# One-hots of a segment sum made one block earlier in a graph layer on one core

## What is computed

```python
h = node_features @ W_node.T + b_node
e = edge_features @ W_edge.T + b_edge
msg = (h[src] + e) @ W_msg.T + b_msg
s = segment_sum(msg, dst, num_segments=n)
deg = segment_sum(ones, dst, num_segments=n)
x = layernorm(x + s / maximum(deg, 1.0)[:, None])
```

## Time and profile before

| | us |
|---|---|
| median of 3 runs | 785.0 (783.43 to 785.41) |
| the profiled execution, its own time | 783.87 |
| its span, first to last instruction | 782.0 |
| TensorE busy (matmul) | 688.6 |
| VectorE busy | 630.1 |
| ScalarE busy | 438.3 |
| GpSimd busy | 270.0 |

### The profile page before, as it was taken

How to read it: one execution, slowest core, us unless ns; L and a number is a source line. 1 busy time by engine, 2 the same in 40 slices (tenths; PEclk the granted TensorE clock), 3 DMA queues, 4 the chain that set the end, 5 groups by cost and what they waited for, 6 DMA issues and landing times.

```text
span 782.0 us, 24842 instructions
## 1 busy us (share of the span) xinstructions
PE 688.6 (88%) x10360; PEld 620.7 (79%) x10360; DVE 630.1 (81%) x1155; ACT 438.3 (56%) x897; POOL 270.0 (35%) x210
## 2 busy tenths in 40 slices
PE   3265577899999989999999998999999999999995
PEld 3244466778888979989988987988998998989994
DVE  7989896868998878878878877789798788779822
ACT  3322496656565556556556555656665665656641
POOL 2737300301443836426426455532543542000000
PEclk9998698999999999999999999999999999999998
DMA  6953543434556574474472575464574574454000
GB/s 174 321 182 79 138 135 111 167 111 146 183 190 194 187 260 156 160 258 158 159 262 55 184 253 195 152 229 156 194 238 146 192 236 153 173 182 169 17 14 16
DMA packets 81518, 130.71 MB, mean 167 GB/s; under 512 B 12100, under 2 KB 25126, under 8 KB 81303
## 3 DMA queue, kind: packets, MB, share of 16 engines
q1 hardware_dynamic: 73230, 115.79, 44.3%
q0 software_dynamic: 7200, 12.39, 5.7%
q10 hardware_dynamic: 974, 0.90, 0.5%
HBM read 125.80 MB, written 3.23 MB: 165 GB/s over the span
## 4 chain that ended last, share of the span: by engine, by line
PE 52%; DVE 11%; issue 4%; POOL 2%; DMA 1%; DVEq 1%; ACT 0%; POOLq 0%
PE x_ps L745 29%; PE count_ps L730 10%; PE win_ps L666 8%; DVE key_hot L886 3%; DVE row_hot L886 2%; PE win_ps L673 2%; POOL x_gathered L607 2%; DMA x_gathered<-in_x_dram,x_index 1%; PE misc_ps L761 1%; PE misc_ps L762 1%; DVE y L932 1%; DVEq L863 1%; DVE y L925 1%; DVE onehot L852 1%; DVE sums_e L876 1%
## 5 line engine op out<-in xcount | busy, mean ns | idle before, releaser
L1416 ACT CAST region<-count_ps 128x490 bf16<-128x490 f32 x575 | 324.3, 573 | 192.8 <-PE count_ps L730 188.5
L745 PE MATMUL x_ps<-region,x_rest 128*128 128x250 bf16 x2254 | 413.6, 270 | 0.0
L745 PE MATMUL x_ps<-region,x_hi 128*128 128x250 bf16 x1127 | 306.2, 272 | 0.5 <-ACT region L1416 0.5
L607 POOL DMA_INDIRECT x_gathered<-in_x_dram,x_index x144 | 195.1, 1355 | 278.5 <-PE count_ps L730 258.9
L886 DVE TENSOR_TENSOR row_hot<-iota_bf,row 125x3200 bf16<-125x3200 bf16 x115 | 209.4, 1821 | 42.1 <-PE count_ps L730 29.1
L730 PE MATMUL count_ps<-key_hot,row_hot 125*128 125x98 bf16 x2875 | 224.4, 209 | 15.2 <-ACT region L1416 8.6
L745 PEld LDWEIGHTS x_ps<-region,x_rest 128*128 128x128 bf16 x2254 | 211.4, 98 | 16.2
L730 PEld LDWEIGHTS count_ps<-key_hot,row_hot 125*128 125x128 bf16 x2875 | 185.6, 99 | 37.9 <-issue 10.4
L886 DVE TENSOR_TENSOR key_hot<-iota_bf,key 125x2500 bf16<-125x2500 bf16 x115 | 167.2, 1454 | 0.0
L666 PE MATMUL win_ps<-edges,onehot 128*32 128x128 f32 x3232 | 107.2, 286 | 13.7 <-DVE onehot L852 12.1
L745 PEld LDWEIGHTS x_ps<-region,x_hi 128*128 128x128 bf16 x1127 | 109.5, 97 | 8.0 <-ACT region L1416 0.6
(11 more groups left out here) (194 smaller groups left out, 415.7 us busy)
## 6 DMA issues: line engine op xcount, KB each, us to landing
edges<-in_edge_attr_dram SPq DMA_DIRECT2D x101, 1024.0 KB, 5.8
resid<-in_x_dram SPq DMA_DIRECT2D x25, 125.0 KB
out_dram<-y SPq DMA_DIRECT2D x25, 125.0 KB
x_gathered<-in_x_dram,x_index POOLq DMA_INDIRECT x144
region<-in_dst_dram ACTq DMA_DIRECT2D x1, 768.0 KB
win_src<-in_src_dram,clipped_int POOLq DMA_INDIRECT x23, 4.4
x_index<-in_src_dram SPq DMA_DIRECT2D x9, 8.0 KB, 5.7
region<-in_L_gnn_W_node_dram SPq DMA_DIRECT2D x1, 64.0 KB
```

Source lines behind the costliest of these rows:

```text
L607: pool.indirect_dma_start(out=x_gathered[:, i, :], out_offset=None, in_=x[:, :], in_offset=bass.IndirectOffsetOnAxis(ap=x_index[:, k, i:i ...
L745: mm = pe.matmul(x_ps[m % 2][:, 0:NB], rows, counts[m % 2][:, b, :], start=(n == 0), stop=(n == PARTS - 1))
L1416: act.copy(counts[m % 2][:, :, f * FILL * 2:(f + 1) * FILL * 2], count_ps[fill % COUNT_BANKS][:, 0:FILL * KEYS].rearrange("p (n b) -> p b ...
```

## The change

In VectorE's list, the limit up to which a segment makes one-hots goes from two blocks past the segment's last one to three, in all segments from u = LEAD on. In the five segments of the lead-in it stays as it was. The number of buffers, the waits written into `make_onehot` and everything else are unchanged.

```diff
@@ -1186,7 +1186,7 @@
                     placed[0] += 1
                 if n is not None:
                     take_stats(n)
-                while ts and hot[0] < min(NS, ts[-1] + ONEHOT_SLOTS):
+                while ts and hot[0] < min(NS, ts[-1] + 1 + (ONEHOT_SLOTS if u >= LEAD else ONEHOT_SLOTS - 1)):
                     make_onehot(hot[0])
                     hot[0] += 1
                 if n is not None:
```

## The result

The changed kernel takes 779.0 us (median of 5 runs, 778.87 to 781.72) where the kernel before, here of five runs too, takes 785.0. By these medians 6.0 us are gained where 9.0 were forecast, and the time lies inside the range of 773.4 to 779.6, at its upper end. The ratio of the two kernels, 0.9940 with a 95% interval of 0.9919 to 0.9962, is that of their means, 779.8 and 784.5 us: 4.7 us gained, which would put the time at 780.3, just above the range. The profiled execution is the slowest of the five, 781.72 us, so by the profiles alone the gain is 783.87 - 781.72 = 2.15 us.

A forecast was written before the change was run, and what follows sets the result against it. TensorE was taken to bound the kernel from 162 us on. Gain 9.7 us less 0.7 for the early one-hot makes 9.0: 783.87 becomes 774.9, plus 1.1 for the median gives 776.0, range 773.4 to 779.6.

The forecast's parts named there:

- What bounds the kernel: From 162 to 775 us TensorE, busy 591.8 of 613 us; before that, other waits hold the kernel.
- (a): VectorE's raised limit makes one-hots earlier, so TensorE's nine one-hot waits at source blocks, 12.1 us, disappear.
- (b): In VectorE's one-hot loop the raised limit adds no wait, so nothing is queued behind a new one.
- The seven places: Source blocks where gathered rows have room: the full one-hot waits are gained, 12.1 - 1.38 - 1.04 = 9.7 us.
- Rival 1: VectorE's additions hide behind the one-hot at seven places: some 3.5 us lost, 779.5; 8 in 100.
- The early one-hot: The third one-hot in the first pair's segment delays L1213, for which TensorE waits: costs 0.7 us, between 0 and 2.2.
- I count both at nothing: Two source blocks where TensorE also awaits gathered rows: waits merge to 2.11 and 2.64 us, no gain.
- Rival 3: Merged waits at two places each bring a half-clock stretch: 1.7 to 3.3 us lost each, about 781; 6 in 100.
- rival 2: All nine places give their full wait, gathers at two coming relatively earlier: 2.4 us more, 773.6; 5 in 100.
- rival 4: Half clock after the merged waits lasts 20 us, as at 73 to 93 us: 796, slower; 3 in 100.
- rival 5: The awaited one-hot is still the late one; only the early 0.7 us is left: 785.7; 4 in 100.
- TensorE's busy time within 1 us: Sign in the next profile: TensorE's busy time, 688.6 us before, is unchanged within 1 us.

The follow-up runs named there:

- after_2: The changed kernel measured once more, on a chip of the quicker sort, against the kernel before: 778.9 us against 785.77, ratio 0.9920.
- selective_2: The changed kernel, but with the old one-hot limit around source blocks 1 and 5, against the kernel before: 778.81 us, ratio 0.9907.
- onehot_later: The changed kernel with the higher one-hot limit only from round 3 on, against the kernel before: 780.13 us, ratio 0.9927.

## Why the prediction was wrong, point by point

- What bounds the kernel, and (a), right: TensorE from 162 us on; the nine waits for one-hots, 12.1 us, are gone, every one.
- (b) No new wait behind the limit: right. No wait for additions or second-level sums appeared, and VectorE's busy time is 629.4 against 630.1.
- The seven places, 9.7 us: right, 9.9 by the rounds. Rival 1 (the additions) did not happen: nothing waits in their place.
- The early one-hot, 0.7 us: right. The three one-hots stand in one row of 4.87 us (some 5 forecast), and the wait for L1213 is 9.1 (9.2).

```profile
81.61 4.87 DVE L852 TENSOR_TENSOR onehot<-iota_bf,rel_col 128x512 f32<-128x512 bf16 x3
```

- The step that failed is "I count both at nothing". Its working was that the gathers end where they ended and TensorE merely waits for them longer: 2.11 and 2.64 us. The prediction's sum lets these two places gain nothing and lose nothing; they lost 3.9 to 7.4 us. The working held for the landing (5.27 us after the last issue, in the row below, against 5.37 in the earlier trace rows) and not for the issues ahead of it. The chain of waits, 272 to 280 us:

```profile
272.34 1.07 POOL x_gathered L607
273.40 0.30 issue
273.71 5.27 DMA x_gathered<-in_x_dram,x_index
```

  The 16 issues became 1.37 us longer, since TensorE's release moved against VectorE. I had read in the earlier trace rows that GpSimd is released by TensorE's counts, and had seen that its issues vary from 0.94 to 2.2 us, but took the variation as given. It depended on the very phase that the change shifts. The waits were 3.45 and 3.57 us. That the extra 1.37 us are gathers that meet one-hots is read from the rows of each gather; no run took it away by the release alone.
- Rival 3 was given 6 in 100 and came true: the clock fell at both places in the first profile, for 6.9 us each, up to 3.05 and 2.65 us lost, and at one in after_2, for 3.4 us, 1.7 lost. Its price of 1.7 to 3.3 us a place was right; its sum was not, since 6.6 us on top of 776.0 is up to 782.6 and not 781. I had the clock at 1.00 after 2.09 us and at 0.50 after 4.53 and put merged waits of 2.1 and 2.6 on the safe side. With waits of 3.5 us there was no safe side; and selective_2 shows that even 1.42 and 1.26 us, 1 us apart, were not on it. The length of the wait doesn't decide alone, since 3.18 and 3.31 us kept the clock; what does is not shown. The chance was too low for a wait that lay between the two rows.
- The two together take 3.9 us (after_2) to 7.4 us (the first profile) of the 9.0 forecast, and leave 5.1 to 1.6; the medians say 6.0 and 6.9. Within the 1 to 2 us by which runs differ that is the whole of the shortfall. That the median still lies in the range is luck: the range was left wide for the spread of runs and for rivals 1 and 2, and neither happened. Rivals 2, 4 and 5 did not happen: no stretch of 20 us at half clock came into the late stage. The early stage of this execution has one that the kernel before doesn't show (49.6 to 70.1 us), but round 5 begins only 0.7 us later, so it cost next to nothing.
- "TensorE's busy time within 1 us": wrong, 4.6 more, which is the half clock seen from the other side. It is all in the stretch from 162 to 775 (596.6 against 591.8 in the earlier trace rows).

## What to carry to other kernels

When a wait is removed from one engine, its signals come earlier against every other engine: for each queue that they release, look at what runs there at the new time, and take no instruction's length as fixed if it varied in the trace before. Where the removed wait stood ahead of another one, add the two, and if the sum lies between a wait that kept the clock and one that lost it, price the half clock as likely. Then give room to what is late next (here source blocks further apart), and the first gain comes whole.

## What the runs showed of the hardware

- A gather issued by GpSimd while VectorE is inside a wide one-hot, an operation with two SBUF inputs, ended 0.81 to 0.83 us after it in 118 of 131 cases (before and changed kernel). A free one takes 0.94 us. Of the 195 us of gathers in the kernel before, 144 x 0.94 = 135 would be free time; 57 of the other 60 us are this.
- Of seven waits for gathered rows those of 3.45 and 3.57 us brought 6.9 us at half clock each, those of 4.06, 3.67 and 2.47 brought 3.4 us, and those of 3.18 (after_2, at 483.4) and 3.31 (onehot_later) none. Two waits of 1.42 and 1.26 us, with 1.1 us of sums between them, brought 3.4 us.
- The same kernel takes 785 us on some chips and 795 on others. On the latter, TensorE has 20 to 27 short stops of 0.3 us or so ahead of its window sums, 5.9 to 10.9 us in all, and all engines of the core stop together for up to 3.6 us where gathers are dense. What does it is open.
